# Attention of a macaron layer: position scores are read back in pairs, behind two writes

## The reference

```
q, k, v = (xn @ W + b).reshape(B, S, H, dh) for each;  p = (pe @ Wp).reshape(S, H, dh)
content = einsum('bihd,bjhd->bhij', q + u_bias, k)
pos     = einsum('bihd,jhd->bhij', q + v_bias, p)
pos     = relative_shift(pos)
attn    = softmax((content + pos) * scale)
out     = einsum('bhij,bjhd->bihd', attn, v).reshape(B, S, D) @ Wo + bo
```

## Time and profile before

| | |
|---|---|
| median of three runs | 3573.16 us |
| the profiled execution | 3570.63 us, span 3568.8 us, granted clock 0.989 |
| busy, share of the span | PE 94%, ACT 65%, DVE 51%, POOL 35% |
| DMA over the span | 1221.81 MB, 342 GB/s |
| writes and reads of scores | 1024 each, 512 KB, median 7.7 and 7.8 us from issue to landing |
| DVE totals (L776) | 1024, 1225 ns each |

### The profile page before, as it was taken

How to read it: one execution, slowest core, us unless ns; L and a number is a source line. 1 busy time by engine, 2 the same in 40 slices (tenths; PEclk the granted TensorE clock), 3 DMA queues, 4 the chain that set the end, 5 groups by cost and what they waited for, 6 DMA issues and landing times. The chain is left out here.

```text
span 3568.8 us, 85700 instructions
## 1 busy us (share of the span) xinstructions
PE 3338.3 (94%) x24380; PEld 1826.7 (51%) x24380; DVE 1811.5 (51%) x3599; ACT 2310.6 (65%) x3253; POOL 1241.6 (35%) x1212
## 2 busy tenths in 40 slices
PE   7996999999999999999999999999999999999988
PEld 5673444444444444444444444444444444444467
DVE  6871444444444444444444444444444444444457
ACT  2443676676776667666666667776767676776633
POOL 1111333333333333333333333333333333333310
PEclk9997999999999999999999999999999999999989
DMA  4655999999999999999999999999999999999962
GB/s 147 204 186 196 372 377 371 376 373 373 374 377 374 376 374 374 372 375 372 375 373 371 372 370 376 372 375 375 377 374 371 377 372 372 377 376 375 339 184 100
DMA packets 439308, 1221.81 MB, mean 342 GB/s; under 512 B 59360, under 2 KB 143840, under 8 KB 439264
## 3 DMA queue, kind: packets, MB, share of 16 engines
q1 hardware_dynamic: 435824, 1219.72, 94.2%
q10 hardware_dynamic: 3440, 1.53, 0.2%
HBM read 624.38 MB, written 596.65 MB: 342 GB/s over the span
## 5 line engine op out<-in xcount | busy, mean ns | idle before, releaser
L776 DVE CUSTOM_DVE_ANT_0 at_pos_in<-at_ps_con,at_pos_in 128x1024 f32<-128x1024 f32 x1024 | 1254.1, 1225 | 1583.4 <-PE at_ps_con L664 1353.8
L813 POOL TENSOR_SCALAR at_pos_in<-at_pos_in,at_neg_max 128x1024 f32<-128x1024 f32 x1024 | 1145.5, 1119 | 1906.9 <-DVE at_neg_max L776 1906.9
L744 ACT ACTIVATE at_pos_out<-at_ps_pos 128x1024 f32<-128x1024 f32 x1024 | 1048.9, 1024 | 602.5 <-PE at_ps_pos L664 602.5
L753 ACT ACTIVATE at_prob<-at_ps_turn 128x512 f32<-128x512 f32 x2048 | 1110.7, 596 | 362.6 <-PE at_ps_turn L687 362.6
L664 PE MATMUL at_ps_con<-at_right,at_left 32*128 32x512 f32 x4096 | 1156.2, 640 | 149.3 <-DVE at_neg_max L776 147.3
L687 PEld LDWEIGHTS at_ps_turn<-keep_ident,at_pos_in 128*128 128x128 f32 x8192 | 898.7, 143 | 628.7 <-issue 426.8
L664 PE MATMUL at_ps_pos<-at_right,at_left 32*128 32x512 f32 x4096 | 1163.7, 644 | 25.8 <-DMA at_right<-scratch_pos_rows 17.9
L687 PE MATMUL at_ps_turn<-keep_ident,at_pos_in 128*128 128x128 f32 x8192 | 1113.7, 279 | 2.3
L699 PE MATMUL at_ps_pv<-at_prob,at_v_aug 128*32 128x512 f32 x4096 | 545.3, 605 | 0.8 <-issue 0.8
L664 PEld LDWEIGHTS at_ps_con<-at_right,at_left 32*128 32x128 f32 x4096 | 308.2, 183 | 341.2 <-ACT at_pos_out L744 196.7
L710 PEld LDWEIGHTS at_ps_head<-keep_fold,at_head_T 128*128 128x128 f32 x2048 | 247.8, 191 | 195.7 <-DVE at_head_T L784 148.6
(11 more groups left out here) (85 smaller groups left out, 1227.6 us busy)
## 6 DMA issues: line engine op xcount, KB each, us to landing
scratch_scores<-at_pos_out SPq DMA_DIRECT2D x1024, 512.0 KB, 7.7
at_pos_in<-scratch_scores SPq DMA_DIRECT2D x1024, 512.0 KB, 7.8
at_left<-scratch_qk_rows SPq DMA_DIRECT2D x512, 64.0 KB, 5.2
scratch_qk_rows<-fr_qk SPq DMA_DIRECT2D x48, 512.0 KB, 5.8
fr_x<-in_L_attn_x_dram SPq DMA_DIRECT2D x16, 512.0 KB, 6.1
scratch_x<-fr_x_bo SPq DMA_DIRECT2D x16, 512.0 KB, 3.2
scratch_values<-fr_values SPq DMA_DIRECT2D x8, 1024.0 KB, 5.2
at_right<-scratch_pos_rows SPq DMA_DIRECT2D x256, 32.0 KB, 5.9
```

What stands on the lines that cost most here:

```text
L744: act.activation(pos_out[:, t.slot, :], ps_pos[:, :, :].rearrange("p a m -> p (a m)"), ACT.Copy)\
L753: act.activation(prob[t.t // QUAD % 2][:, 4 * n:4 * n + 4, k * P:(k + 1) * P], ps_turn[:, n, :].rearrange("p (j i) -> p j i", i=P), ACT.Exp)\
L776: dve.tensor_tensor_reduce(pos_in[:, t.slot, :], ps_con[:, :, :].rearrange("p a m -> p (a m)"), pos_in[:, t.slot, :], -SCALE, 3.0e38, ALU. ...
L813: pool.tensor_scalar(pos_in[:, t.slot, :], pos_in[:, t.slot, :], -1.0, neg_max[:, t.slot:t.slot + 1], ALU.mult, ALU.add).then_inc(shifted, 1)
```

## The change

At even steps SP now only writes. At odd steps it writes tile t+8 and then reads back two tiles, t+3 and t+4, one behind the other. So the order in the queue goes from write, read, write, read to write, write, read, read. The prologue does the same. Nothing else is changed: the same transfers, buffers and waits.

```diff
--- before.py
+++ after.py
@@ -635,9 +635,10 @@
                     if w.i == 0 and Tile(r, t + LEAD + TILES).real():
                         load_qv(Tile(r, t + LEAD + TILES))
                     write(w)
-                back = Tile(r, t + LEAD - READ_LAG)
-                if back.real():
-                    read_back(back)
+                if t % 2 == 1:
+                    for back in (Tile(r, t + LEAD - READ_LAG - 1), Tile(r, t + LEAD - READ_LAG)):
+                        if back.real():
+                            read_back(back)
                 if t % TILES == 1 and Tile(r, t - 1 + TILES).real():
                     load_qk(Tile(r, t - 1 + TILES))
                 done = Tile(r, t - TILES)
@@ -650,7 +651,8 @@
             load_qk(Tile(0, 0))
             for w in range(LEAD):
                 write(Tile(0, w))
-                if w >= READ_LAG:
+                if w > READ_LAG and w % 2 == 1:
+                    read_back(Tile(0, w - READ_LAG - 1))
                     read_back(Tile(0, w - READ_LAG))
             rounds(sp, step)
             for k in range(2):
```

## The result

| | before | after |
|---|---|---|
| median (range) of 4 runs each | 3573.34 us (3572.06 to 3575.43) | 3891.11 us (3885.21 to 3905.68) |
| ratio, 95% interval | | 1.0895 (1.0864 to 1.0925) |
| profiled execution | 3570.63 us, span 3568.8 | 3892.48 us, span 3890.7, granted clock 0.983 |

The change makes the kernel slower by 8.9%. The direction was forecast, the size was not: 318 us in place of 38.

A forecast was written before the change was run, and what follows sets the result against it. The PE, DVE, PE chain at 23.82 us a unit was taken as the bound, transfers just in time. Late even reads, 127 x 0.30 = 38 us, on 3570.6 gave 3609 (3611 by the median); it named 3608, range 3568 to 3660.

The forecast's parts named there:

- What bounds the kernel now: Attention loop: the chain PE, DVE, PE sets the pace at 23.82 us a unit; transfers are just in time.
- No instruction and no byte is added; the waits cost nothing: SP's queue: still 1024 writes and 1024 reads of 512 KB; waits before reads ask for nothing later, taken at nothing.
- The moment at which its n-th piece lands doesn't change when two pieces swap places: Non-empty queue: a moved even read lands when the write it swaps with landed; read 6 1.07 us late in the mean.
- How often it is paid: Lateness of read 6 over 127 units: between 25 and 90 us, taken as 0.30 us a unit, 38 us.
- 0.36 us of cover: PE's other work at the even tiles' steps hides 0.36 us of a late DVE total, leaving 0.71 for read 6.
- Even tiles: Sign in the loop: DVE's wait for reads rises from 111.8 us to several hundred and sits on even tiles.
- tile 6 first: Part of that sign: among the even tiles, DVE's waits for reads show on tile 6 of the unit first.
- Faster: Rival: fewer turns between writes and reads shorten packets and DVE's waits; 11 us less, 3562 us; chance 0.08.
- Shift once: Rival: engines slip one or two us in the first units, then reads are in time; 3575 us; chance 0.24 including hidden.
- it doesn't do what it says: Rival: where SP is late, only the order changes; same as shifting once for reads 4 and 6; no chance of its own.
- Paid in full: Rival: SP's loads renew the lateness each unit; 3663 us, or 3692 by the first unit's figure; chance 0.16 including more.

The follow-up runs named there:

- e5: Kernel before the change with score rows of 1024 numbers in place of 1025 (no relative shift): 3568.15 us, ratio 0.9954 to the kernel before.
- e14: Changed kernel with both reads of the odd step moved ahead of that step's write: 3745.06 us, ratio 1.0478 to the kernel before.
- m1: Transfers alone, no engine computing, 512 KB writes and reads in several orders, with rows of 1025 or 1024: pairs carry 10 to 12% less than in turn with 1025.
- e3: Kernel before with READ_LAG 5 for 4, so write and read in turn but every read one step later: 3810.41 us, ratio 1.0664 to the kernel before.
- m4: Transfers alone, rows of 1025, at most 3, 4 and 6 in flight: in turn 297, 364, 405 GB/s; pairs 277, 337, 351.
- e13: Changed kernel with LEAD 10 for 8 and rows of 1024 numbers: 3642.42 us, ratio 1.0177 to the kernel before.
- e10: Changed kernel with its nine small loads spread over steps 0, 1, 2 and 4 of the unit: 3692.09 us, ratio 1.0317 to the kernel before.
- e11: Changed kernel with small loads spread over steps 0, 1, 2 and 4 and rows of 1024 numbers: 3689.26 us, ratio 1.0297 to the kernel before.
- e12: Kernel before, write and read in turn, with small loads spread over steps 0, 1, 2 and 4, as control: 3609.22 us, ratio 1.0088.
- m3: Transfers alone, at most 5 in flight, other row distances and placings: pairs with rows 1089 apart 399 GB/s, neighbouring partitions on neighbouring rows 322.

## Why the prediction missed the size

- **"What bounds the kernel now": right.** The chain of PE and DVE at 23.82 us, transfers just in time. In e5 transfers get easier and the unit stays at 23.81.
- **"No instruction and no byte is added; the waits cost nothing": right** (1024 of each, 8.9 MB a unit). In e14, where the wait for a write did come nearer, it showed.
- **"The moment at which its n-th piece lands doesn't change when two pieces swap places": the step that failed.** By it read 6 would land where write 3 landed, 20.96 us after write 7; it lands 22.37 us after it, and each unit pays these 1.4 us. It fails for two reasons. First, write 7 waits for the engines and can't move forward, so behind it read 6 stands two issues further down, where the rule counts one (18 in place of 16: read 2 as well as write 3): it is issued 14.83 us after write 7, write 3 was at 13.80. Second, the rate isn't a property of the queue alone; it is one of the order too, 389 against 343 GB/s for in turn and pairs with these rows (m1). So read 6, though issued later, takes 7.54 us to land where write 3 took 7.16; in e3, with the same 18 issues but in turn, it takes 6.80 and lands 21.37 us after write 7. The rate was taken for granted from a share of 1.02 that stays at 1.03 when the rate falls by 10%. How much of the last 1.0 us, from 21.37 to 22.37, is the order's alone no run here divides.
- **"How often it is paid" and "0.36 us of cover": wrong as well.** I took 0.30 us a unit, as the engines slip until the queue is short enough. They slip with the queue: write 7 waits for the engines, and everything to read 6 hangs on write 7. Following that loop from write 7 to the next one, in means over units 3 to 125: 13.03 (SP from write 7 to read 6) + 6.25 (read 6's landing) + 0.55 (to DVE's start of tile 6) + 4.02 (to the next write 7) = 23.85 before, and 14.83 + 7.54 + 0.29 + 3.76 = 26.42 after. So SP's stretch brings 1.80 us, the slower landing 1.29, and only 0.52 comes back from what was slack, less than the 0.77 of slack and 0.36 of cover that the forecast read from one unit. Put by its own terms: the swap moves read 6 back by 1.68 us (19.28 to 20.96) less 0.52, so 1.16 us a unit even by its rule, where 0.30 was taken; the other 1.40 are the step above. With a shorter queue the landing does fall, as I supposed (reads 6.6 us in e3), but so does the rate (m4), and the slip isn't undone: the unit there is 25.75.
- **Even tiles: right.** DVE's waits for reads on them, the odd ones with more time; "tile 6 first" wasn't, all four stand at 0.20 to 0.33 us. The direction came out for the reason given, an even read late behind one more write.
- **The rivals.** "Faster", by fewer turns of direction, is the reverse of what happened: 397 GB/s in turn, 356 in twos and 379 in fours. "Shift once" is out, and so is "it doesn't do what it says". "Paid in full" (3663 to 3692) named the reason why slipping doesn't help, and the sign named for it, a unit of 24.5 us or more, is what came; but its price, 90 to 119 us, is 28 to 37% of the measured 318: 0.71 to 0.94 us a unit, where 2.53 were paid.
- **The Trainium skill's** "Rules for kernel authors" in "DMA: Bandwidth & Descriptors" (issue early, wait late) was the right warning: one step of lead less costs 6.6% (e3). The 3.2 us for a transfer, by the Trainium skill's "Anatomy of one DMA" on the same page, was no help: reads take 8.1 us at the median here.

How the 318 us divide can't be said in one sum, as the repairs overlap: 155 us go with the rows, 226 with more lead, 199 with spread loads. **Open:** why adjoining rows make the rate depend on the order; and how much the order costs with round rows. With at most 4 in flight these carry 374 GB/s in turn and 354 in pairs alone (two more stretches of m4), with 5 both 419 to 420, so some effect of the order is left when the queue is short. The 1.8% that e13 keeps, with two steps more of lead, aren't explained. PE hardly waits for small loads in e10 and e11, so the 0.9% of e12 can't simply be taken off theirs. No version that keeps the relative shift was better than the kernel before.

## What to carry to other kernels

Before reordering DMAs in a queue that is full, measure the rate of the new order alone: a few lines of transfers without compute showed in one run the 10% that the argument on positions missed. Read GB/s beside the busy share, since the share is full at either rate. And where the queue's next issue hangs on the engine that waits for it, lateness isn't used up once; start at the issue that waits for an engine, count what stands between it and the transfer that is wanted first, and follow the loop round, for that sum is the new period. Such a sum says where the time is, not yet what a repair is worth: the next loop may be close behind.

## What the runs showed of the hardware

- Writes whose rows adjoin at odd places (1025 numbers apart), mixed with reads: 397 GB/s in turn, 356 in twos, 379 in fours, without a limit; rows of 1024, with at most 5 in flight: 420 and 419; rows 1089 apart in twos 399. Neighbouring partitions on neighbouring rows, in twos: 322 (m1, m3).
- The rate by the number of 512 KB transfers in flight, in turn, rows of 1025: 3: 297 (281 in another run), 4: 364, 5: 389 (381, 399), 6: 405 GB/s (m1 to m4). The DMA share is under 1 only for 3 of them (0.93, 0.86).
- A full DMA share hides slower packets: one of 4096 bytes takes 175 ns before and 195 after in the loop, 171 in turn and 197 in pairs alone, at shares of 1.02 to 1.05.
- SP issues large transfers back to back at 0.7 to 0.8 us from start to start, and nine small loads in a unit of 26 us were worth 199 us of 3891 by their place alone (e10).
